# A gated attention and feed-forward block on one core: VectorE's scores ahead of its row statistics, and TensorE's small products and first rows moved

## The reference

```python
def _L0_xattn_ref(query, key, value, w_q, w_k, w_v, mask):
    q = jnp.einsum('bsd,dh->bsh', query, w_q)
    k = jnp.einsum('bsd,dh->bsh', key, w_k)
    v = jnp.einsum('bsd,dh->bsh', value, w_v)
    scores = jnp.einsum('bqh,bkh->bqk', q, k) * scale
    scores = jnp.where(causal, scores, -jnp.inf)
    attn = jax.nn.softmax(scores, axis=-1)
    out = jnp.einsum('bqk,bkh->bqh', attn, v)
    return out
...
def _L0_ffn_ref(x, W1, b1, W2, b2):
    h = jnp.einsum('bsd,fd->bsf', x, _ternary(W1)) + b1
    h = jax.nn.gelu(h, approximate=False)
    out = jnp.einsum('bsf,df->bsd', h, _ternary(W2)) + b2
    return out
x = x + jnp.tanh(g_xattn[0]) * _L0_xattn_ref(_layernorm(x, axis=-1), ctx_1024, ctx_1024, L0_xattn_w_q, L0_xattn_w_k, L0_xattn_w_v, 1)
x = x + jnp.tanh(g_ffn[0]) * _L0_ffn_ref(_layernorm(x, axis=-1), L0_ffn_W1, L0_ffn_b1, L0_ffn_W2, L0_ffn_b2)
```

## Time and profile before

| | before |
|---|---|
| median of 3 runs | 1702.15 us (1699.64 to 1705.04) |
| the profiled execution, its own time | 1701.67 us |
| its span | 1699.5 us |
| PE busy | 1639.5 us (96%), 8492 matmuls |
| DVE busy | 886.0 us (52%) |
| ACT busy | 655.4 us (39%) |
| POOL busy | 302.5 us (18%) |
| mean granted clock of TensorE | 0.985 |

### The profile page before, as it was taken

How to read it: one execution, slowest core, us unless ns; L and a number is a source line. 1 busy time by engine, 2 the same in 40 slices (tenths; PEclk the granted TensorE clock), 3 DMA queues, 4 the chain that set the end, 5 groups by cost and what they waited for, 6 DMA issues and landing times.

```text
span 1699.5 us, 23723 instructions
## 1 busy us (share of the span) xinstructions
PE 1639.5 (96%) x8492; PEld 837.7 (49%) x8492; DVE 886.0 (52%) x1598; ACT 655.4 (39%) x1032; POOL 302.5 (18%) x330
## 2 busy tenths in 40 slices
PE   8699899999999999999999999999999999999998
PEld 4455555555555555554444444444444444444444
DVE  6656556565656557768434444444434444344432
ACT  2332332423233245422444444444444444344443
POOL 1211111111111111112211221122211221122110
PEclk9899999999999999999999999999999999999999
DMA  6445354453545469755222122212221122212210
GB/s 186 118 94 141 90 143 97 113 121 89 148 89 142 98 153 241 196 144 151 58 65 65 25 71 64 65 22 74 68 62 44 49 68 68 62 25 71 66 37 25
DMA packets 261798, 157.50 MB, mean 93 GB/s; under 512 B 222432, under 2 KB 222432, under 8 KB 260448
## 3 DMA queue, kind: packets, MB, share of 16 engines
q1 hardware_dynamic: 260432, 154.21, 35.3%
q10 hardware_dynamic: 1296, 2.37, 0.4%
HBM read 70.53 MB, written 33.55 MB: 61 GB/s over the span
## 4 chain that ended last, share of the span: by engine, by line
PE 76%; DVE 11%; issue 5%; DMA 3%; ACT 3%; SPq 2%; POOL 0%; DVEq 0%; POOLq 0%
PE s_ps L1057 13%; PE e_ps L1057 13%; PE s_ps L985 7%; PE o_ps L921 7%; PE t_ps L921 7%; PE v_ps L921 7%; PE m_ps L921 7%; PE o_ps L1014 6%; PE t_ps L947 6%; PE v_ps L966 5%; DMA x_ring<-in_x 2%; DVE cmax L647 2%; SPq L267 1%; DVE x_ring L777 1%; DVE w_s L815 1%
## 5 line engine op out<-in xcount | busy, mean ns | idle before, releaser
L859 DVE SCALAR_TENSOR_TENSOR v_s<-g,sc,v_s 128x512 f16<-128x512 f32 x256 | 246.6, 968 | 385.6 <-ACT v_s L535 381.9
L1057 PE MATMUL s_ps<-w_s,v_s 128*128 128x512 f16 x1024 | 262.8, 379 | 0.0
L1057 PE MATMUL e_ps<-w_s,v_s 128*128 128x512 f16 x1024 | 262.8, 379 | 0.0
L947 PE MATMUL t_ps<-xnT,a_s 128*128 128x256 f16 x1512 | 189.8, 286 | 16.5 <-issue 16.5
L985 PE MATMUL s_ps<-ctx_s,tT 128*128 128x512 f16 (+3 forms) x1152 | 199.4, 328 | 5.1 <-DVE tT L699 5.1
L454 ACT ACTIVATE p<-s_ps,ebias,esc 128x128 f32<-128x128 f32 (+3 forms) x64 | 53.2, 831 | 390.3 <-DVE ebias L746 390.3
L1014 PE MATMUL o_ps<-v_s,pT 128*128 128x512 f16 x864 | 198.6, 381 | 2.8 <-DVE x_ring L777 2.8
L535 ACT ACTIVATE v_s<-g,sc 128x512 f16<-128x512 f32 x256 | 184.7, 721 | 8.4
L966 PE MATMUL v_ps<-wv_s,ctx_s 128*128 128x512 f16 x768 | 178.6, 382 | 2.8 <-ACT ctx_s L444 2.6
L947 PEld LDWEIGHTS t_ps<-xnT,a_s 128*128 128x128 f16 x1512 | 154.3, 103 | 44.5 <-issue 14.3
L1057 PEld LDWEIGHTS e_ps<-w_s,v_s 128*128 128x128 f16 x1024 | 100.2, 98 | 120.8
(11 more groups left out here) (113 smaller groups left out, 1537.8 us busy)
## 6 DMA issues: line engine op xcount, KB each, us to landing
x_ring<-in_x SPq DMA_DIRECT2D x64, 256.0 KB, 2.9
out_y<-x_ring SPq DMA_DIRECT2D x64, 256.0 KB, 2.2
raw<-out_y SPq DMA_DIRECT2D x64, 256.0 KB, 3.2
out_y<-v_s SPq DMA_DIRECT2D x64, 256.0 KB, 2.1
raw<-in_ctxT SPq DMA_DIRECT2D x7, 2048.0 KB, 8.7
w_in<-in_w1T SPq DMA_DIRECT2D x16, 512.0 KB, 3.9
w_in<-in_w2T SPq DMA_DIRECT2D x16, 512.0 KB, 4.8
raw<-in_ctxT SPq DMA_DIRECT2D x2, 1024.0 KB, 14.8
```

The lines of the kernel that those rows point to most:

```text
L859: v.scalar_tensor_tensor(out=g_s[:, f % 4, LO], in0=g32[:, f % 2], scalar=col(C_SG), in1=g_s[:, f % 4, HI], op0=ALU.mult, op1=ALU.subtract ...
L947: last_mm = mm(bank[:, dd], a_s[:, aa, c, d * P:(d + 1) * P], xnT[:, pr, xa, c, :], start=(n == 0 and c == 0), stop=(n == 2 and c == DC - 1))
L1057: last_mm = mm(y_ps[i], g_s[:, f % 4, a, i * P:(i + 1) * P], w2_s[:, f, :], start=(f == 0 and a == HI), stop=(f == FC - 1 and a == LO))
```

## The change

It has eight parts. (1) In a slot DVE takes mask, maximum and bias of the scores first, and then waits for the x tile and does bn_stats. (2) In a slot PE's spread_ctx and totals come behind T and V instead of ahead of them. (3) In the prologue the two gates, b1 and b2 are loaded from POOL's queue instead of ACT's, b1 with a semaphore of its own; x tiles 2 and 3 are loaded ahead of ctx; the rows of tiles 2 to 4 are normalized on POOL (`first_rows`), with their statistics on DVE earlier, and ACT's order follows; T(0) goes to bank e_ps and stands ahead of V(-1) and slot 0. (4) `W_PLAN` has a second ternary step in slot 56 and one less in slot 62. (5) The tiles of the feed-forward part are loaded at the end of slot 56 (`BODY - 8`). (6) The last PV goes to bank e_ps, so it doesn't wait for DVE's update from o_ps, and hidden(3) stands ahead of it, which waits for that update. (7) The feed-forward loop does y(F) and then hidden(F+4), which with the fourth hidden product ahead of the loop is the same sequence of products. (8) `LN_STEPS` is (0, 2, 4, 7) instead of (1, 3, 6, 9).

```diff
-                  NT - 9: "TSS", NT - 8: "T", NT - 7: "T", NT - 6: "T", NT - 5: "T", NT - 4: "TT", NT - 3: "TT",
-                  NT - 2: "TT", NT - 1: "TT"}
+                  NT - 9: "TSS", NT - 8: "TT", NT - 7: "T", NT - 6: "T", NT - 5: "T", NT - 4: "TT", NT - 3: "TT",
+                  NT - 2: "T", NT - 1: "TT"}
...
-        LN_STEPS = (1, 3, 6, 9)
+        LN_STEPS = (0, 2, 4, 7)
...
+            if s == 0:
+                return e_ps[:, 0:D].rearrange("p (a n) -> p a n", a=2)
...
+        def o_bank(last, s):
+
+            return e_ps[:, 0:D] if last and s == BODY else o_ps[:, :]
...
+            load_x(2)
+            load_x(3)
...
-                if s == BODY - 6:
+                if s == BODY - 8:
...
+            g.dma_start(b1_s[:, :], b1c).then_inc(b1_in, 16)
+            g.dma_start(col(C_G0), g_xattn.partition_broadcast(P)).then_inc(small_in, 16)
+            g.dma_start(col(C_G1), g_ffn.partition_broadcast(P)).then_inc(small_in, 16)
+            g.dma_start(b2_row[:, :], b2.partition_broadcast(P)).then_inc(small_in, 16)
...
+            def first_rows(k):
+
+                r = k % 2
+                pool.wait_ge(ln_var, k + 1)
+                g.tensor_tensor(rstd[:, r:r + 1], var_s[:, r:r + 1], minus_half[:, :], ALU.pow).then_inc(ln_rstd, 1)
+                pool.wait_ge(ln_rstd, k + 1)
+                g.tensor_scalar(xn32[:, r], x_ring[:, k], mv[:, r, 0:1], rstd[:, r:r + 1], ALU.subtract,
+                                ALU.mult).then_inc(xn_ready, 1)
+                pool.wait_ge(xn_ready, k + 1)
+                pool.wait_ge(xn_hi, k + 1)
+                pool.wait_ge(x_turned[r], turned_before(0, k - LN_LEAD))
+                g.tensor_tensor(xn_s[:, r, LO], xn32[:, r], xn_s[:, r, HI], ALU.subtract).then_inc(xn_lo, 1)
...
-            act.wait_ge(small_in, 64)
-            a.activation(col(C_TANH0, 2), col(C_G0, 2), ACT.Tanh).then_inc(tanh_done, 1)
             act.wait_ge(a_scaled, 1)
             for m in range(DC):
                 act.wait_ge(a_mm, m + 1)
                 a.activation(a_s[:, HI, m], a_ps[m], ACT.Copy, scale=col(C_SA)).then_inc(a_hi, 1)
+                if m == 1:
+                    rows_upper(0, -3)
+            rows_upper(0, -2)
...
+                if live:
+
+                    dve.wait_ge(s_mm, t + 1)
+                    diag = s_ps[:, i * P:(i + 1) * P]
+                    v.tensor_tensor(diag, diag, causal[:, :], ALU.add).then_inc(s_masked, 1)
+                    dve.wait_ge(s_masked, t + 1)
+                    v.tensor_reduce(negmax[:, r:r + 1], s_ps[:, 0:(i + 1) * P], AX.X, ALU.max,
+                                    negate=True).then_inc(s_max, 1)
...
                 if norm:
                     v.bn_stats(bn6[:, rk], src).then_inc(bn_done, 1)
-                if live:
...
-                if not last or t < NT - T_LEAD:
-                    t_product(it, s)
-                if last and t == NT:
-
-                    pe.wait_ge(w_ternary, NW // 2)
-                    hidden(0, 0, 0)
-                    hidden(1, 1, 0)
-                    hidden(2, 2, 0)
-                if not last or t + 1 < NT:
-                    v_product(it, s)
...
+                    pe.wait_ge(o_done, NT - 1 + O0)
+                    hidden(3, 3, 0)
...
+            t_product(0, 0)
             v_product(0, -1)
             slot(0, 0)
...
-                    if not last or F + 3 < NG * FC:
-                        hidden(F + 3, gg * FC + f + 3, g + (f + 3) // FC)
...
+                    if not last or F + 4 < NG * FC:
+                        hidden(F + 4, gg * FC + f + 4, g + (f + 4) // FC)
```

More of the change, by code:

```diff
@@ L219, in turned_before @@
             return it * BODY * 16 + 16 * ((s + LN_LEAD) - (s + LN_LEAD) % 2)
-        LN_STEPS = (1, 3, 6, 9)
+        LN_STEPS = (0, 2, 4, 7)
         def t_bank(s):
-            return t_ps[:, :, :] if s != -1 else o_ps[:, :].rearrange("p (a n) -> p a n", a=2)
+            if s == -1:
+                return o_ps[:, :].rearrange("p (a n) -> p a n", a=2)
+            if s == 0:
+                return e_ps[:, 0:D].rearrange("p (a n) -> p a n", a=2)
+            return t_ps[:, :, :]
+        def o_bank(last, s):
+            return e_ps[:, 0:D] if last and s == BODY else o_ps[:, :]
         block = es.enter_context(nc.Block())
@@ L242, in _ @@
                              ctx_batches[0][:, 2 * h:2 * h + 2].rearrange("p c s -> p (c s)")).then_inc(ctx_in0[h], 16)
-            for t in range(2, 7):
+            for t in range(4, 7):
                 load_x(t)
@@ L401, in add_bias @@
                 g.tensor_tensor(x2_in[:, u], x2_in[:, u], b2_row[:, :], ALU.add).then_inc(x2_biased, 1)
-            for s in range(FIRST_SLOT, 1):
-                slot(0, s)
+            def first_rows(k):
[9 more added lines that the diff above has]
+                g.tensor_tensor(xn_s[:, r, LO], xn32[:, r], xn_s[:, r, HI], ALU.subtract).then_inc(xn_lo, 1)
+            slot(0, -5)
+            slot(0, -4)
+            first_rows(2)
+            first_rows(3)
+            first_rows(4)
+            slot(0, 0)
             for it in range(TURNS - 1):
@@ L510, in _ @@
             t_upper(0, -2)
+            t_upper(0, -1)
+            act.wait_ge(small_in, 48)
+            a.activation(col(C_TANH0, 2), col(C_G0, 2), ACT.Tanh).then_inc(tanh_done, 1)
             ctx_upper(0, 0, 0)
-            t_upper(0, -1)
-            rows_upper(0, -3)
-            rows_upper(0, -2)
+            rows_upper(0, -1)
             v_upper(0, -1)
             ctx_upper(0, 0, 1)
-            rows_upper(0, -1)
             slot(0, 0)
@@ L715, in first_rows @@
                 ln_variance(k, k % 2)
-                ln_rows(k, k % 2, x_ring[:, k], k >= 2)
+            def first_rows(k):
+                first_stats(k)
+                ln_rows(k, k % 2, x_ring[:, k], False)
             def slot(it, s, last=False):
@@ L776, in slot @@
                     dve.wait_ge(pv_mm, t + PV0)
-                    v.scalar_tensor_tensor(out=x_ring[:, (s - 1) % 8], in0=o_ps[:, :], scalar=osc[:, q:q + 1],
+                    v.scalar_tensor_tensor(out=x_ring[:, (s - 1) % 8], in0=o_bank(last, s), scalar=osc[:, q:q + 1],
                                            in1=x_ring[:, (s - 1) % 8], op0=ALU.mult, op1=ALU.add).then_inc(o_done, 1)
@@ L824, in _ @@
             bound_product()
+            first_stats(2)
             scale_product()
@@ L827, in _ @@
             wv_max()
+            first_stats(3)
             product_lower()
@@ L988, in slot @@
                     last_mm.then_inc(s_mm, 1)
+                if s > 0 and (not last or t < NT - T_LEAD):
+                    t_product(it, s)
+                if last and t == NT:
+                    pe.wait_ge(w_ternary, NW // 2)
+                    hidden(0, 0, 0)
+                    hidden(1, 1, 0)
+                    hidden(2, 2, 0)
+                    pe.wait_ge(o_done, NT - 1 + O0)
+                    hidden(3, 3, 0)
+                if not last or t + 1 < NT:
+                    v_product(it, s)
                 if last and t - 1 in TOTAL_SLOTS:
@@ L1009, in slot @@
                     pe.wait_ge(v_split, t)
-                    pe.wait_ge(o_done, t + O0 - 1)
+                    if not last or t < NT:
+                        pe.wait_ge(o_done, t + O0 - 1)
                     jn, par = (s - 1) % TB, ((s - 1) // TB) % 2
@@ L1013, in slot @@
                         for j in range(jn + 1):
-                            last_mm = mm(o_ps[:, :], pT[:, (s - 1) % 2, pa, j], v_s[:, par, va, j],
+                            last_mm = mm(o_bank(last, s), pT[:, (s - 1) % 2, pa, j], v_s[:, par, va, j],
                                          start=(n == 0 and j == 0), stop=(n == 2 and j == jn))
```

39 lines of the change are left out of this document (13 added, 26 removed).

## The result

| | before | after |
|---|---|---|
| median | 1701.24 us (4 runs beside it) | 1658.65 us (1657.12 to 1659.3, 4 runs) |
| the profiled execution, its own time | 1701.67 us | 1659.3 us |
| its span | 1699.5 us | 1657.5 us |
| PE idle in the span | 60.0 us | 31.9 us |
| mean granted clock of TensorE | 0.985 | 0.994 |

The change makes the kernel faster: the ratio is 0.9745 (95% interval 0.9727 to 0.9763), 42.6 us between the medians. I forecast 1663 us, in a range from 1651 to 1676. The first y, forecast at 770 us, starts at 769.41, and behind it 888.1 us pass instead of the 891 forecast.

What follows compares the result with a forecast made beforehand. PE is busy for 96% of the span, so only its 60 us idle and low-clock stretches can be won. 47.7 us won less 9.2 lost gives 38.5, from 1701.67 to 1663 us, range 1651 to 1676.

Steps and rivals of the forecast that it cites:

- Batches, 30.3 + 1.3 us: Slot 3 on, six batches: the small product's waits and their clock cost go, 30.3 us; the first wait adds 1.3.
- The margin of 0.3 us at the scores of slot 4: Batches: DVE's lower half of T(3) is ready at 180.2 us, 0.3 us ahead of PE, so no wait.
- rival B: Short slots: DVE becomes the bound, 1.5 to 2.5 us wait before slot 4's scores; 1675 to 1681 us; chance 0.17.
- Prologue, 5.0 us: Start of the kernel: next ctx load and T(2) come 5 us earlier, T(0) runs at 35 us; 5.0 us won.
- the bound of 4 us: Prologue: most that POOL's four loads could cost if one takes twice as long as the longest; nothing was taken.
- Slots 56 to 64, 9.7 + 1.4 us: End of attention: waits and slow clock go, 9.7 us in slots 56 to 60, 1.4 in slots 61 to 64.
- The second wait: Last batch: PE's 4.12 us wait for DVE's lower half of T(59), said to go with the earlier feed-forward load.
- The feed-forward part, 9.2 us lost: Heads of groups: y waits for DVE's lower half, 7.7 us over 14 groups, 1.45 for the first; 9.2 us lost.
- The formula: Heads of feed-forward groups: PE waits B - Y - 3.3 us, 0.1 to 1.7 us for each.
- B - Y: Feed-forward group: from start of y(0) to first bn_stats, when its tile lands; DVE's wait for the tile plus 0.66 us.
- Rival A: Feed-forward part loses nothing, as if PE had more in hand than one lower half; 1654 us; chance 0.14.

Runs made afterwards that it cites:

- Parts 1 and 2 alone: The kernel before with the two reorders of the slot (DVE's and PE's) and nothing else: 1657.5 us, ratio 0.9722.
- The ten runs with six waits of 3.4 to 4.75 us: The changed kernel with spread_ctx back ahead of T and V and bn_stats first again: 1701.61 us (1690.49 to 1706.21), ratio 0.9974.

## Why the prediction came out right, point by point

**Batches, 30.3 + 1.3 us: 33.55 us and a part of the prologue's 5.6.** The mechanism was as described, and both halves of it were shown by undoing them. The size was off by 3 us because the undisturbed round takes 88.61 us with the small product in it (spreads at 84.00 and 172.61) and not 89.0, and because the 1.0 us wait for turned rows left the stretch for the slot behind it (0.82 us at 622.07). The margin of 0.3 us at the scores of slot 4 measured 0.4; rival B lost by that much, and with part 1 undone its waits come, 0.4 to 2.0 us in six batches.

**Prologue, 5.0 us: at most 4.7.** T(-2) at 27.12 and T(0) at 36.70 us came near the forecast (26.75 and 35), the next ctx load at 58.05 us against 57.2. What I took too low is POOL's work: its tensor_scalar takes 2.08 us for a tile's rows. ACT waited 6.98 us for those of tile 4 ahead of the upper half of V(-1), and so V(0) waits 2.80 us and takes 4.44; with ACT's order turned round it waits 0.83 us and takes 2.75. POOL's four loads took 0.5 to 0.8 us each. They put PE's first weight product back by 2.1 us, of which 0.4 were left at T(-2), so the bound of 4 us was not reached.

**Slots 56 to 64, 9.7 + 1.4 us: 9.2.** Here the number was near and the attribution wrong. The step "The second wait is there because DVE waited 4.91 us for the load of the first feed-forward tile, which now comes two slots earlier" gave to part 5 what happens without it, with parts 1 and 2 alone. Parts 4 to 6 together win nothing measurable (10.7 us without them, 9.2 with). The wait of 2.31 us in slot 58 of this profile goes with the load of part 5, which stands ahead of turned rows in SP's queue: no profile with the later load has it. But with the load at the same place and both reorders the others show 0.25 us or none, so it depends on when transfers land, and the queue as its cause is likely and not shown. I had named DVE's side of that load and not the queue's.

**The feed-forward part, 9.2 us lost: 6.4.** The formula held: in the second group B - Y is 830.63 - 825.83 = 4.80 us, which gives 1.5, and y waited 1.32 us. Its input was off: the sum of B - Y over 14 groups, taken as 53.9 us from the earlier trace rows, is 51.5 in this run, so 5.3 us, and 1.0 for the first group. (The list of PE's waits has 4.4 us of it, since it leaves out the shortest waits.) B - Y isn't fixed, since it is when a DMA lands: with the prologue of before, 1660.2 - 769.27 = 890.9 us passed behind the first y, a loss of 9.2 us. Of the chain, 1.0 us is DVE's lower half beside POOL's addition, 1.72 us against 0.75 for the one before it, at 831.45. POOL's addition ends at 837.07 us and the lower half, begun beside it at 835.89, at 837.61. Without the addition it took 0.75 us, and the loss fell from 6.4 to 0.8 us. Rival A is ruled out: undoing part 8 gives back 7.5 us.
The Trainium skill (SBUF — State Buffer, SBUF: two separate sides) says that the pair of ports shared by VectorE and GpSimd is an exclusive lock, held for a whole instruction. The rows agree: the half ends 0.54 us behind the addition's end.

By terms the sum was off by 3.3 us in the batches and 2.8 in the feed-forward part on the one side, and by 0.7 and 1.9 in the prologue and the last slots on the other, with one cause misplaced. That the sum came within 3.5 us of the 42.0 between the spans is in part luck: these errors cancel, and the feed-forward part alone differs by 2.8 us from one profile to the next. Parts 1 and 2 alone won 45.2 us between the spans, more than the whole change; part 3 adds some 0 to 4.7, part 8 takes 6 to 9 away, and parts 4 to 6 are not seen.

## What to carry to other kernels

When two edits take away the same wait, undo each and also try each alone: a sum over parts gives the gain to one of them by the order in which it is told. Move the small instruction that waits behind the long ones that don't, and then look at once at what is late next and how much it has in hand; here undoing the second cost 13 us beside 23 for the first, and undoing both 43. And before an operation that waits for a load is moved ahead of one that the bound engine reads, compare the longest of those waits with what that engine has in hand; here it was 4.8 us against 3.3.

## What was not expected of the hardware

A tensor_scalar of 128x512 float32 with two per-row operands takes POOL 2.08 us, and DVE 0.54; POOL's tensor_tensor of the same size takes 1.16. Waits of PE of the same length have different consequences: in one execution (part 2 undone) T took 4.02 us at a granted clock of 0.67 behind a wait of 2.77 us (at 449.51 us), and 2.78 us at 1.00 behind another of 2.77 us (at 542.39). So a wait near 3 us can't be priced with certainty. The ten runs with six waits of 3.4 to 4.75 us scatter by 16 us; with both reorders, four or five runs of a kernel scatter by 0.8 to 3.7 us, and by 7 in the one with the load at the end of slot 58.
